# Moving rows from partition to partition in four SBUF-to-SBUF transfers, and sending the probabilities of two early tiles that way as well

## What is computed

```python
mod = (silu(c) @ wmod).reshape(4, 6, 1, 512)
sa, ca, ga, sb, cb, gb = (mod[:, i] for i in range(6))   # gates ga, gb: magnitude at least 0.25
h  = layernorm(x) * (1 + ca) + sa
x1 = x + ga * attention(h)
h2 = layernorm(x1) * (1 + cb) + sb
out = x1 + gb * ffn(h2)

def attention(h):            # 16 heads, scores of rank 64
    q, k = h @ Wq.T, h @ Wk.T
    scores = einsum('hr,bir,bjr->bhij', ones, q, k)      # the same for every head
    return (softmax(scores) @ (h @ Wv.T)) @ Wo.T
def ffn(h2):                 # 8 factors of 512x512
    return einsum('btd,rde->bte', h2, factors) / sqrt(8) + bias
```

## Time and profile before

| what | before |
|---|---|
| time, median of 3 runs | 449.67 us (448.71 to 452.26) |
| the profiled execution: its time, its span | 449.63 us, 447.8 us |
| PE busy | 439.6 us, 98% |
| DVE busy | 356.6 us, 80% |
| ACT busy | 320.0 us, 71% |
| POOL busy | 234.9 us, 52% |
| granted TensorE clock, mean | 1.00 (the 2.4 GHz level) |
| transfers by hardware queue q1 | 80.51 MB, 73872 packets |

### The profile page before, as it was taken

The page is one execution under the profiler, slowest core; times in us unless marked ns, Lnnn a source line. Parts: engine busy times, 40 slices in busy tenths (PEclk is TensorE's granted clock), DMA queues, the critical chain, the costliest instruction groups (busy, mean ns, idle before and its releaser), DMA issues.

```text
span 447.8 us, 7294 instructions
## 1 busy us (share of the span) xinstructions
PE 439.6 (98%) x2118; PEld 361.6 (81%) x2118; DVE 356.6 (80%) x610; ACT 320.0 (71%) x642; POOL 234.9 (52%) x308
## 2 busy tenths in 40 slices
PE   8899999999999999999999999999999999999996
PEld 7586888878888888788888888888888888887885
DVE  5787557868887887988897878888886777999977
ACT  3677557778797786678877787779777664667651
POOL 0554516852555643356565544456564527177982
PEclk9999999999999999999999999999999999999999
DMA  8999986533665457667676367766686146658423
GB/s 308 393 388 287 256 156 115 120 121 108 204 210 184 133 159 217 205 210 235 209 243 201 117 200 221 234 187 215 187 254 198 47 140 203 200 172 278 131 79 141
DMA packets 77750, 88.05 MB, mean 197 GB/s; under 512 B 5000, under 2 KB 55944, under 8 KB 77200
## 3 DMA queue, kind: packets, MB, share of 16 engines
q1 hardware_dynamic: 73872, 80.51, 56.4%
q0 software_dynamic: 3264, 6.29, 7.9%
q10 hardware_dynamic: 576, 0.79, 0.5%
HBM read 53.49 MB, written 34.10 MB: 196 GB/s over the span
## 4 chain that ended last, share of the span: by engine, by line
PE 77%; DVE 9%; issue 4%; POOL 3%; ACT 3%; DMA 3%; SPq 0%; DVEq 0%; POOLq 0%; ACTq 0%
PE ps_o L525 9%; PE ps_o L527 9%; PE ps_o L526 9%; PE ps_v L525 5%; PE ps_v L526 5%; PE ps_v L527 5%; PE ps_y L525 4%; PE ps_y L527 4%; PE ps_y L526 4%; PE ps_qk L525 3%; PE ps_qk L526 3%; PE ps_qk L527 3%; PE ps_s L614 2%; PE ps_s L615 2%; PE ps_t L531 1%
## 5 line engine op out<-in xcount | busy, mean ns | idle before, releaser
L1685 POOL TENSOR_SCALAR ve<-mv 128x1 f32<-128x1 f32 x64 | 17.0, 266 | 160.0 <-DVE mv L1320 119.3
L525 PE MATMUL ps_o<-v_lo,pt_hi 128*128 128x512 f32 x192 | 74.9, 390 | 1.0 <-DVE pt_lo L1205 0.9
L526 PE MATMUL ps_o<-v_hi,pt_lo 128*128 128x512 f32 x192 | 74.8, 389 | 0.0
L527 PE MATMUL ps_o<-v_hi,pt_hi 128*128 128x512 f32 x192 | 74.8, 389 | 0.0
L1205 DVE TENSOR_TENSOR h_lo<-h_f,h_hi 128x512 fp32r<-128x512 f32 x57 | 41.6, 730 | 29.0 <-ACT h_hi L843 28.7
L871 ACT ACTIVATE h_f<-x1b,mod_t 128x128 f32<-128x128 f32 x120 | 52.9, 594 | 3.8 <-DVE x1b L1338 3.8
L1687 POOL TENSOR_TENSOR rstd<-ve,minus_half 128x1 f32<-128x1 f32 x64 | 45.8, 716 | 5.3
L525 PEld LDWEIGHTS ps_o<-v_lo,pt_hi 128*128 128x128 f32 x192 | 36.0, 188 | 9.3 <-issue 1.8
L525 PE MATMUL ps_v<-wvo_lo,h_hi 128*128 128x512 f32 x108 | 43.1, 399 | 0.3 <-DVE h_lo L1205 0.3
L919 ACT ACTIVATE probs<-ps_s,negmax 128x1024 f32<-128x1024 f32 x32 | 35.4, 1108 | 10.0 <-DVE negmax L1264 9.7
L526 PE MATMUL ps_v<-wvo_hi,h_lo 128*128 128x512 f32 x108 | 42.2, 391 | 0.0
(11 more groups left out here) (238 smaller groups left out, 1193.2 us busy)
## 6 DMA issues: line engine op xcount, KB each, us to landing
x_blocks<-xn SPq DMA_DIRECT2D x50, 256.0 KB, 2.8
p_blocks<-probs SPq DMA_DIRECT2D x24, 512.0 KB, 3.8
pb<-p_blocks SPq DMA_DIRECT2D x96, 128.0 KB, 2.7
...
result<-x_ring SPq DMA_DIRECT2D x15, 512.0 KB, 3.0
...
```

Of the source, the lines that this page charges most:

```text
L525: nc.tensor.matmul(acc, a_hi, b_lo, start=first, stop=False)
L526: nc.tensor.matmul(acc, a_lo, b_hi, start=False, stop=False)
L527: return nc.tensor.matmul(acc, a_hi, b_hi, start=False, stop=last)
L1685: nc.gpsimd.tensor_scalar(ve[:, one], mv[:, u, 1:2], EPS, None, ALU.add).then_inc(ve_done, 1)
```

## The change

1. The DRAM tensors go. `to_blocks` moves rows of xn straight into xb or x1b in four transfers, one for each quarter of columns (128 source partitions to 32 destination partitions); `move_p` does the same from probs to pb. One set of four takes the place of a send and a fetch.
2. Because such a transfer puts rows 4c to 4c+3 on partition c, `in_quarters` is now `(c b)`: pt_hi and pt_lo are written (and pt_hi read by DVE) with a step of four float32.
3. Waits on the send's end become waits on the landing of the four transfers: of xn in ACT's normalizations, of probs in the exponentials.
4. On SP a move of x for tile t+10 stands in step t, where before the send stood there and the fetch a step later; the move of the probabilities stands where the send stood.
5. LAST_EARLY is 2 instead of 4: the probabilities of tiles 3 and 4 go by the transfers and DVE's turn; PE no longer transposes them, and the order of scores, queries, maxima and exponentials of the first steps moves with it.
6. In DVE's prologue both parts of h of tile 0 stand ahead of the moments of tile 2; on POOL `of_x` of tile 12 stands between the second and third of the four `factor_rest`.

```diff
-LAST_EARLY = 4
+LAST_EARLY = 2
...
         def in_quarters(tile):
-            return tile.rearrange("p k (b c) -> p k b c", b=Q)
+            return tile.rearrange("p k (c b) -> p k b c", b=Q)
...
+            def to_blocks(to, rows, loaded):
+                for a in range(Q):
+                    sp.dma_start(to[BLK * a:BLK * (a + 1), :], rows[:, P * a:P * (a + 1)]).then_inc(loaded, 16)
+
+            def move_x(q):
+                wait_alone(sp, sp_passed, xn_done, q + 1)
                 wait_alone(sp, sp_passed, h_f_done, q)
-                blocks_in(xb, x_blocks[u], xb_loaded)
+                to_blocks(xb, xn, xb_loaded)
+
+            def move_x1(t):
+                wait_alone(sp, sp_passed, x2n_done, t + 1)
+                if t > 0:
                     wait_alone(sp, sp_passed, h2_f_done, t)
-                blocks_in(x1b, x1_blocks[u], x1b_loaded)
+                to_blocks(x1b, xn, x1b_loaded)
...
+            def move_p(t):
                 n = trips_of(t)
                 sp.wait_ge(exp_done, t + 1)
...
                 sp.wait_ge(pt_lo_done, 2 * (t - 1))
                 for a in range(Q):
-                    sp.dma_start(pb[BLK * a:BLK * (a + 1), n & 1, :].rearrange("c (b x) -> c b x", b=Q),
-                                 p_blocks[n & 1, a].rearrange("(b c) x -> c b x", b=Q)).then_inc(pb_loaded, 16)
+                    sp.dma_start(pb[BLK * a:BLK * (a + 1), n & 1, :],
+                                 probs[:, KEYS // Q * a:KEYS // Q * (a + 1)]).then_inc(pb_loaded, 16)
...
             def normalize_x_blocks(q, u):
                 act.wait_ge(nmr1_done, q + 1)
-                act.wait_ge(x2n_out, 16 * (q - TB - 2))
+                act.wait_ge(x1b_loaded, 16 * Q * (q - TB - 2))
...
                 elif t:
-                    act.wait_ge(p_out, 16 * trips_of(t))
+                    act.wait_ge(pb_loaded, 16 * Q * trips_of(t))
...
                 elif after_x:
-                    act.wait_ge(xn_out, 16 * (t - 1))
+                    act.wait_ge(xb_loaded, 16 * Q * (t - 1))
                 else:
-                    act.wait_ge(x2n_out, 16 * t)
+                    act.wait_ge(x1b_loaded, 16 * Q * t)
...
             def turn_x1(t):
-                dve.wait_ge(x1b_loaded, 16 * (t + 1))
+                dve.wait_ge(x1b_loaded, 16 * Q * (t + 1))
...
+            h_first(0)
+            h_second(0)
             moments_of(2)
-            h_first(0)
             wvo_rest(0)
-            h_second(0)
             wvo_rest(1)
...
-            for k in range(C):
-                pool.wait_ge(f_hi_done, k + 1)
-                nc.gpsimd.tensor_tensor(f_lo[:, k, :], f_sum[:, k, :], full(f_hi[:, k, :]),
-                                        ALU.subtract).then_inc(f_lo_done, 1)
+            factor_rest(0)
+            factor_rest(1)
             of_x(TB + 4, 0)
+            factor_rest(2)
+            factor_rest(3)
             of_x1(2, 0)
```

More of the change, by code:

```diff
@@ L93, in adaln_block @@
     gate_rows = nc.dram_tensor("gate_rows", [2, B, D], F32, kind="Internal").ap()
-    x_blocks = nc.dram_tensor("x_blocks", [2, Q, P, P], F32, kind="Internal").ap()
-    x1_blocks = nc.dram_tensor("x1_blocks", [2, Q, P, P], F32, kind="Internal").ap()
-    p_blocks = nc.dram_tensor("p_blocks", [2, Q, P, KEYS // Q], F32, kind="Internal").ap()
     with ExitStack() as ctx:
@@ L406, in _ @@
             spread_gate(1, 0)
-            def blocks_out(blocks, rows, done, count, out_sem):
-                wait_alone(sp, sp_passed, done, count)
-                sp.dma_start(blocks.rearrange("a p x -> p a x"),
-                             rows[:].rearrange("p (a x) -> p a x", a=Q)).then_inc(out_sem, 16)
-            def blocks_in(to, blocks, loaded):
-                sp.dma_start(to[:], blocks.rearrange("a (c b) x -> (a c) (b x)", b=Q)).then_inc(loaded, 16)
-            def send_x(q, u):
-                blocks_out(x_blocks[u], xn, xn_done, q + 1, xn_out)
@@ L477, in _ @@
                 step(t)
-            send_p(25)
-            fetch_p(25)
-            send_p(26)
-            send_x1(23, 1)
-            fetch_p(26)
-            fetch_x1(23, 1)
-            send_p(27)
-            send_x1(24, 0)
-            fetch_p(27)
-            fetch_x1(24, 0)
-            send_p(28)
-            fetch_p(28)
-            send_p(29)
-            send_x1(25, 1)
-            fetch_p(29)
-            fetch_x1(25, 1)
-            send_x1(26, 0)
-            send_p(30)
-            fetch_x1(26, 0)
+            move_p(25)
+            move_p(26)
+            move_x1(23)
+            move_p(27)
+            move_x1(24)
+            move_p(28)
+            move_p(29)
+            move_x1(25)
+            move_x1(26)
+            move_p(30)
             store_pair(10)
-            fetch_p(30)
-            send_p(31)
-            send_x1(27, 1)
+            move_p(31)
+            move_x1(27)
             store_pair(11)
-            fetch_x1(27, 1)
-            fetch_p(31)
-            send_x1(28, 0)
-            fetch_x1(28, 0)
-            send_x1(29, 1)
-            fetch_x1(29, 1)
+            move_x1(28)
+            move_x1(29)
             store_pair(12)
@@ L1768, in sum_factors, with factor_rest @@
                 nc.gpsimd.tensor_tensor(f_sum[:, k, :], f_sum[:, k, :], g_sum[:, k, :], ALU.add).then_inc(f_summed, 1)
+            def factor_rest(k):
+                pool.wait_ge(f_hi_done, k + 1)
+                nc.gpsimd.tensor_tensor(f_lo[:, k, :], f_sum[:, k, :], full(f_hi[:, k, :]),
+                                        ALU.subtract).then_inc(f_lo_done, 1)
             def last_wv_rest():
```

47 lines of the change are left out of this document (13 added, 34 removed).

## The result

The change makes the kernel slower by 5.4%: 473.75 us, median of 4 runs (472.32 to 475.75), against 449.42 (448.71 to 452.26, 4 runs) before; the ratio is 1.0538, 95% interval 1.0507 to 1.0568. 456.4 was forecast, with 461 as the upper end of the range. The profiled execution took 472.32 us for a span of 470.5, so 1.82 us lie around it, as before.

What follows compares the result with a forecast made beforehand. PE was taken to set the pace everywhere, with DVE full too in the last eight tiles. 447.8 + 1.3 + 0.3 - 0.8 + 6.0 = 454.6, with 1.83 around it 456.4 us; range 447 to 461.

Steps and rivals of the forecast that it cites:

- What bounds the kernel: Whole kernel: PE, busy 439.6 of 447.8 us, sets the pace everywhere; in the last eight tiles DVE is full too.
- The price of the step: Halves of pt with the 16-byte step: 0.43 us more on ACT, 0.53 us more on DVE for each half tile.
- Rival A: Halves of pt: DVE writes with a step at full rate, only ACT pays; 450.7 us, chance 26%.
- The last eight tiles: Tiles 25 to 31: 14 longer DVE halves, 7.4 us against 2.25 us left, make PE lose 6.0 us.
- The middle: From 190 to 355 us DVE's idle time covers its longer halves save +0.3; pauses behind DVE's wait at 170.68 go, -0.8.
- Rival C: Each step: x1 transfers come onto ACT's path, 0.4 us in some 13 steps, 5 us; 461 us, chance 12%.
- The early tiles: Tiles 2 to 4: tile 3 ready 3.0 us later, less 0.9 for scores and 0.8 for PE's transposes: +1.3 us.
- Prologue and POOL: Start and tile 12: DVE's moved h of tile 0 gives 0 (-1.0 to +0.3), POOL's moved of_x 0.
- The sum: Whole kernel: the terms add to 454.6 us, with 1.83 around it 456.4 us, 1.5% slower.

Runs made afterwards that it cites:

- e5: The changed kernel with the loop order turned, so pt_hi and pt_lo are written contiguously and pb is read with a step of 1024 bytes: 477.37 us.
- e12: The kernel before with the 16-byte step on DVE's writing of pt_lo alone, ACT writing pt_hi without it: 457.46 us, ratio 1.0165.
- e2: The kernel before with in_quarters as in the change, so pt_hi and pt_lo get the 16-byte step, transfers still through DRAM: 461.14 us, ratio 1.0262.
- e1: The changed kernel with in_quarters as before, so pt_hi and pt_lo are written without a step: 466.79 us, 1.0401 of before.
- e4b: The changed kernel with a tile of its own for the normalized rows of x1, in the memory of the bias: 467.11 us, 1.0385 of before.
- e6: The kernel before with x and x1 in direct transfers of four, probabilities still through DRAM, nothing else of the change: 459.30 us, ratio 1.0218.
- e3: The changed kernel with LAST_EARLY 4 again, so PE transposes tiles 3 and 4: 468.47 us.
- e10: The kernel before with LAST_EARLY 2 alone, so tiles 3 and 4 go through DRAM and DVE's turn: 449.36 us, ratio 0.9990.
- w1: The kernel before with POOL's new order alone (of_x of tile 12 between the second and third factor_rest): 449.14 us, ratio 0.9983.
- e7: The kernel before with the change's orders in DVE's prologue and on POOL alone: 450.69 us, ratio 1.0026.

## Why the prediction was wrong, step by step

**What bounds the kernel.** Right: PE had nothing to spare, and each wait that grew showed.

**The price of the step.** Right in kind, near in size. DVE 0.39 us for half a tile (1.08 us, the row below, instead of 0.69) where 0.53 was taken; ACT 0.49 (1117 against 623 ns) where 0.43 was taken.

```profile
390.33 1.08 DVE L1163 TENSOR_TENSOR v_lo<-pb,v_hi 128x512 fp32r<-128x512 f32 x1 [0.62 <-ACT v_hi L801]
```

The rule of 16-byte lines (the Trainium skill, SBUF — State Buffer, section "Door 1: The DMA port swizzle (why `[64,N]` ≈ `[32,N]`)"), that each access which crosses to a new line pays, agrees: both engines pay, and, as e5 shows, on reading too. Rival A falls: DVE alone cost 7.7 us in e12. With it falls what the prediction had read out of another page of the Trainium skill. VectorE: DVE Perf Modes, section "Mode 1× (REGULAR) — the baseline", gives one result a cycle and says that fp32 and odd strides work in this mode; at a step of 16 bytes that rate does not hold here, by the row above (1.08 us against 0.69).

**The last eight tiles, +6.0.** Near in number, in part by luck. With the measured 0.39 us the prediction's own sum gives 14 x 0.39 = 5.5, less 2.25 of idle time at least 3.2; e2 lost 3.9 in that stretch, and 2.5 more behind it, which the prediction had not. The change lost 7.4 there and nothing behind it, and only part of it by the step: without the step (e1) 3.7 are left, where ACT waits for landings. Some is the clock: in the profiled execution of the change PE paused for 2.46 us ahead of 436.05, and from 436 to 440 us the granted clock was 0.57. Matmuls started up to 0.43 us apart there, which is the 1.2 GHz level, instead of 0.23: ten of them took 3.95 us instead of 2.3. (In e1 and e4b a stretch of 4 us in the last tiles shows the like, 0.67 and 0.62; in e2 and e6 none does.) The loss as a whole is not the clock's: the slowest run, 475.75 us, had a mean granted clock of 1.000.

**The middle, +0.3 - 0.8.** This step failed, with 9.4 us lost. Two errors in it. First, DVE's 1.06 us a tile was set against its idle time (2.2 us a tile). That lies behind a chain which DVE's halves of pt themselves delay, through POOL's moments of x1 and ACT's rows (shown under e2), so it was no room: e2 loses 5.7 us there. Second, SP's sets and their landings on xn were costed at nothing: e6 loses 2.0 us there, and e1, which has all of the change but the step, 6.0. The two overlap: taken out of the change, the step gives back 3.4 us in these tiles and the single xn 4.1. DVE's wait of 2.04 us for pb, on which the -0.8 rested, is gone in the change; what that gave can't be told beside the rest.

**Rival C** was the mechanism that had been missing, with 12% and 461 us, and was too small. It counted one wait a step, for x1 (4.0 to 5.1 us from the end of L871 on, 4.7 us of room); in the change there are two, the rows of x after those of x1 and the other way round:

```profile
251.05 0.81 ACT L904 ACTIVATE xn<-x_ring,nmr,rstd 128x512 f32<-128x512 f32 x1 [2.51 <-DMA xb<-xn]
...
257.80 0.82 ACT L837 ACTIVATE xn<-x_ring,nmr,rstd 128x512 f32<-128x512 f32 x1 [1.55 <-DMA x1b<-xn]
...
253.63 2.48 SPq L408 DMA_DIRECT2D x1b<-xn  x4
...
255.76 0.69 DVE L1163 TENSOR_TENSOR h_lo<-h_f,h_hi 128x512 fp32r<-128x512 f32 x1 [3.10 <-ACT h_hi L801]
...
256.51 0.39 PE L483 MATMUL ps_qk<-h_lo,wqk_hi 128*128 128x256 f32 x1 [1.36 <-DVE h_lo L1163]
```

The four issues take 2.48 us where 1.74 was read from the earlier trace rows, so SP, costed at nothing, is part of the way: issue at 253.63, xn free at 257.8. It is so for the rows of x too, which in the change stand behind the probabilities:

```profile
243.90 0.82 ACT L837 ACTIVATE xn<-x_ring,nmr,rstd 128x512 f32<-128x512 f32 x1
...
243.37 2.48 SPq L426 DMA_DIRECT2D pb<-probs  x4
246.03 2.48 SPq L408 DMA_DIRECT2D xb<-xn  x4
```

The rows are written at 244.72, and SP comes to them 1.3 us later; by estimate, had SP been free, the wait of 2.51 us at 251.05 would be about half. In 16 of the change's 20 sets of x SP was the last to be ready, in e6 in none. From the end of the rows to the landing, the median in the middle (113 to 345 us) is 5.3 us for x and 5.8 for x1 in the change, 4.3 and 5.9 in e6, 2.6 and 4.2 before. No run moved the probabilities behind x again, so what this order costs is not shown. ACT's wait of 2.51 us ahead of 251.05 passes through h_f and h_hi to DVE (3.10) and to PE (1.36). And that the send had freed xn without waiting for x1b was said in the part on the early tiles, but not carried to the middle and the last eight tiles.

**The early tiles, +1.3.** The chain was right in each link (exponentials ahead of pt_hi, L829 late, the set of x1 behind it, xn, tile 3): 4.7 us were lost instead. The set took 4.2 us from 96.7 on as worked out (4.0), but exponentials and maximum held ACT up longer (L829 at 94.93, less the 1.2 us that the start was late, against 92.3), and the 1.7 us that PE saves were lost again, 1.2 of them at the two pauses shown under e3 and e10.

**Prologue and POOL, 0.** Right for POOL's order (w1). For DVE's it is open: e7's 1.2 us (0.3 to 2.1) would be outside the bound of +0.3, but it may be the start of the loads.

**The sum.** Alone the parts cost 11.9 (e2), 9.8 (e6), 1.2 (e7) and nothing (e10), 22.9 us; together 24.3. Adding up was not the trouble, as far as these runs tell (the direct transfers of the probabilities are in none of them); the sizes of the terms for the early tiles and the middle were. But what a part gives back when it is taken out of the change is not what it costs alone, since they share ACT's list: 7.0 for the step (e1), 6.6 for the single xn (e4b), and 5.3 for an order that alone is free (e3).
